# A block with deformable convolution and spectral filters: seven fills on GpSimd behind every 18 gathers

## What is computed

```python
n = layer_norm_over_channels(x)
# deformable convolution, 3x3, on n
offset = conv2d(n, offset_w, offset_b)            # 18 channels: where each tap looks
mask   = sigmoid(conv2d(n, mask_w, mask_b))       # 9 channels
# each tap reads four neighbours (y0,x0), (y0,x0+1), (y0+1,x0), (y0+1,x0+1) of a point
# that depends on the data, weighs them bilinearly and by the mask
out = einsum('bcthw,oct->bohw', val, weight)
out = batch_norm(out);  x = x + out * sigmoid(out)
# spectral filters on the tokens of layer_norm(x)
for i, frac in enumerate((1, 2, 4, 8)):           # four branches over the first 1/frac of the tokens
    U_plus, U_minus = causal convolutions of u with 16 filters
    si = sum_k sigma_k**0.25 * (U_plus M_plus[k] + U_minus M_minus[k]) + three lags of u by M_u
out = x + sum of the branches by a softmax choice
```

## Time and profile before

| | us |
|---|---|
| median of 3 runs | 725.98 |
| lowest and highest | 724.54, 726.33 |
| the profiled execution | 725.11 |
| its span, first instruction to last | 723.3 |

### The profile page before, as it was taken

One profiled execution on the slowest core, in us unless ns is written; L12 is line 12 of the kernel. 1 busy time (PEld: TensorE's weight loads), 2 busy tenths in 40 slices (PEclk: granted clock), 3 DMA queues, 4 the chain that ended last, 5 costly groups with the idle time before them and its releaser, 6 DMA issues.

```text
span 723.3 us, 9279 instructions
## 1 busy us (share of the span) xinstructions
PE 493.3 (68%) x3678; PEld 279.6 (39%) x3678; DVE 314.7 (44%) x800; ACT 167.6 (23%) x421; POOL 290.5 (40%) x295
## 2 busy tenths in 40 slices
PE   5977429334733983697459944997238636999998
PEld 3543104222522541254025611565125313565566
DVE  6468320749910980197006650079019701843000
ACT  1112003112401420241023300343024102433322
POOL 1157760450774277237710775007732771000000
PEclk9967557756865995699569965999659956999999
DMA  8525346830232133113310332003321331000000
GB/s 170 124 82 157 106 117 215 263 100 0 86 105 73 30 95 102 44 37 97 106 32 2 88 102 81 1 10 94 106 62 30 102 102 37 8 1 2 9 1 8
DMA packets 43763, 54.03 MB, mean 75 GB/s; under 512 B 24664, under 2 KB 34142, under 8 KB 43721
## 3 DMA queue, kind: packets, MB, share of 16 engines
q0 software_dynamic: 13824, 37.77, 18.0%
q1 hardware_dynamic: 23841, 13.42, 6.8%
q10 hardware_dynamic: 6056, 2.26, 1.3%
HBM read 50.12 MB, written 3.30 MB: 74 GB/s over the span
## 4 chain that ended last, share of the span: by engine, by line
PE 53%; issue 18%; another core or an unknown queue 18%; DVE 4%; ACT 4%; DMA 1%; SPq 1%; DVEq 0%
PE bank L891 28%; PE bank L903 7%; PE bank L836 3%; PE bank L762 2%; PE bank L826 2%; ACT u_conv L662 2%; PE bank L743 1%; PE bank L922 1%; PE bank L734 1%; PE bank L795 1%; PE bank L797 1%; DMA filt<-in_L_ffn_phi_dram 1%; PE bank L847 1%; DVE sil L468 1%
## 5 line engine op out<-in xcount | busy, mean ns | idle before, releaser
L269 POOL DMA_INDIRECT G<-corner_table,idx x288 | 287.9, 1000 | 310.0 <-DVE idx L362 191.3
L891 PE MATMUL bank<-filt,u_hi 128*64 128x512 f16 x1280 | 219.3, 405 | 55.8 <-issue 23.5
L662 ACT ACTIVATE u_conv<-bank,f_scale 128x256 f32<-128x256 f32 x256 | 106.0, 470 | 307.3 <-remote 159.6
L891 PE MATMUL bank<-filt,u_lo 128*64 128x512 f16 x640 | 142.0, 402 | 6.7 <-issue 6.2
L891 PEld LDWEIGHTS bank<-filt,u_hi 128*64 128x64 f16 x1280 | 80.3, 113 | 128.5 <-issue 48.0
L459 DVE TENSOR_TENSOR V<-G 128x576 f32<-128x576 f32 x32 | 24.3, 758 | 189.4 <-PE bank L827 111.6
L903 PE MATMUL bank<-u_conv,mixw 128*64 128x256 f32 (+1 forms) x640 | 87.1, 357 | 26.1 <-issue 25.9
L455 DVE TENSOR_TENSOR G<-G,bank 128x2304 f32<-128x2304 f32 x32 | 81.6, 2549 | 0.3
L903 PEld LDWEIGHTS bank<-u_conv,mixw 128*64 128x64 f32 x640 | 48.8, 144 | 50.7 <-issue 38.5
L891 PEld LDWEIGHTS bank<-filt,u_lo 128*64 128x64 f16 x640 | 43.3, 114 | 46.7 <-issue 19.1
L836 PE MATMUL bank<-vT,w_main 128*64 128x128 f32 (+1 forms) x320 | 26.2, 301 | 44.0 <-issue 40.9
(11 more groups left out here) (158 smaller groups left out, 369.8 us busy)
## 6 DMA issues: line engine op xcount, KB each, us to landing
filt<-filter_rows SPq DMA_DIRECT2D x16, 514.0 KB, 7.9
G<-corner_table,idx POOLq DMA_INDIRECT x288
corner_table<-n_uT SPq DMA_DIRECT2D x12, 128.0 KB, 2.8
mixw<-in_x_dram SPq DMA_DIRECT2D x2, 512.0 KB, 6.1
filt<-in_L_ffn_M_phi_plus_dram SPq DMA_DIRECT2D x8, 128.0 KB, 4.3
out_dram<-o_sb ACTq DMA_DIRECT2D x8, 128.0 KB, 1.9
filt<-n_L_ffn_M_phi_minus_dram ACTq DMA_DIRECT2D x4, 128.0 KB, 4.0
corner_table<-n_uT ACTq DMA_DIRECT2D x4, 128.0 KB, 2.8
```

The lines of the kernel that those rows point to most:

```text
L269: pool.indirect_dma_start(G[:, k, tap, :], None, corners[bp], bass.IndirectOffsetOnAxis(ap=idx[:, q % 2, k, tap:tap + 1], axis=0)).then_in ...
L662: act.activation(u_conv[:, g % 2, k, b2], conv_ps[b2][:, 2 * P * k:2 * P * k + 2 * P].rearrange("c (p a) -> c p a", p=2), ACT.Copy, scale= ...
L891: last = pe.matmul(conv_ps[b2][C * src:C * src + C, :].rearrange("c (k p a) -> c k p a", k=2, p=2), u[:, NJ * bp + j2, b2, src], h, start= ...
```

## The change

Behind the second and the fourth token row of each row q, which is behind 18 gathers each, GpSimd fills a new scratch tile of 128 x 1024 float32 with zeros, seven times. Each fill raises a semaphore, and GpSimd waits for it before the next instruction. That makes 16 times seven fills. Nobody reads the tile.

```diff
+REST, RESTS = 1024, 7
...
+        rest = sb("rest", [P, REST])
...
-        idx_ready = sem("idx_ready")
+        idx_ready, rested = sem("idx_ready"), sem("rested")
...
                                 G[:, k, tap, :], None, corners[bp],
                                 bass.IndirectOffsetOnAxis(ap=idx[:, q % 2, k, tap:tap + 1], axis=0)
                             ).then_inc(gathered[k], 16)
+                        if k % 2:
+                            for i in range(RESTS):
+                                pool.memset(rest[:], 0.0).then_inc(rested, 1)
+                                pool.wait_ge(rested, RESTS * (2 * q + k // 2) + i + 1)
```

## The result

| | before | after |
|---|---|---|
| median, us | 725.26 (4 runs, 721.93 to 726.33) | 697.75 (4 runs, 696.09 to 702.1) |
| ratio of the times, 95% interval | | 0.9637 [0.9582, 0.9693] |
| profiled execution, us | 725.11 | 696.97 |
| its span, us | 723.3 | 695.1 |
| mean granted clock | 0.787 | 0.801 |

The account below looks back on a forecast made before the run. Engines stand still while gathers run; 36% of the chain, about 260 us, shows no releaser. From 725.1 us: less 12 early stage, less 69 rows, plus 9 restarts gives 653; forecast 654 us, range 612 to 702.

Parts of the forecast that it names:

- The reading of what bounds the kernel: Some 19 us into a run of gathers, TensorE, VectorE and ScalarE are held nearly still (the hold); 177 us in six rows.
- The price of the pause: Seven waited fills on GpSimd take 7.7 us; with one issue gap the second 18 gathers come 8.0 us later.
- The second pause costs nothing: Behind k = 3, from 181 us on, the pause lies in GpSimd's wait for indices, 20.4 us at the shortest.
- The stage ahead: From 48.2 us to row 2's start at 181.05: GpSimd gets there at 160, at most 21 us gained, 12 taken.
- The rows: Six rows from 181 us on: two short holds, 18 us together, replace one of 29.5; 69 us back.
- How long there is the open number: How long engines run free into a row's second 18 gathers: 11.8 to 19 us, leaving 15.2 to 22.4 of hold.
- the restarts: Two a row instead of one, matmuls at 1.2 GHz behind each hold: 1.5 us a row, 9 us lost.
- the 4.36 us break ahead of 48.23: Early pause in gathers, after which engines ran at full pace until 60.0; source of the lower bound 11.8 us.
- Full relief: Rival: the pause empties everything, holds are 15.2 us a row, the early stage gives 21; 607 to 632 us, chance 0.18.
- The slower case: Rival: the hold returns as soon as gathers return, 4.7 to 8.0 us more per row; 767 to 798 us, chance 0.11.
- The fills hold VectorE: Rival: fills keep short VectorE operations waiting, 3.8 us for each of 15 pauses, 57 us; 680 to 710 us, chance 0.11.
- and vice versa: Skill rule that DMA and compute cannot slow each other; read as: gathers hold nothing, so a pause gives nothing.

Follow-up runs that it names:

- experiments 6 and 18: One waited fill of 160 elements behind every gather in place of the pauses, against the kernel before: 566.4 us (0.7802), on another chip 563.58 us (0.777).
- experiment 2: The pauses of rows q = 2 to 7 alone, without those of rows 0 and 1, against the kernel before: 715.83 us, 0.9823.
- experiment 3: The changed kernel with 14 fills in a pause instead of seven, against the kernel before: 735.63 against 728.49 us, 1.0134.
- Experiment 9: The kernel before with each gather fetching half of each partition's bytes, no fills: 742.71 against 742.16 us, one run.
- experiment 11: The changed kernel, waiting from row 2 on for four 4 KB SyncE copies instead of fills, against the kernel before: 755.75 us, 1.0175; void as a test.
- 15 to 17: The changed kernel with pauses of 14 fills of 450 elements, 25 of 180, or seven of 1024 again, against the kernel before: 0.9887, 0.9712, 0.9538.

## Why the prediction was right and wrong

**The reading of what bounds the kernel: right, in its form not quite.** The standstill goes with the gathers: with a fill between them that nobody reads, 1.47 us apart instead of 1.25, the long holds go and some 160 us with them (experiments 6 and 18). "What is held is every instruction, one by one" is too strong. In the held stretch from 60 us on VectorE's three long operations on a token row begin one right behind the other (86.07, 88.64, 90.03). And the short waits of a held stretch of before have a regular form that I had not seen:

```profile
82.10 0.15 DVE L291 SCALAR_TENSOR_TENSOR st<-st 64x1 f32<-64x1 f32 x1 [1.25 <-DVE st L290]
...
94.70 0.14 DVE L439 TENSOR_SCALAR f_max<-f_max 16x1 f32<-16x1 f32 x1 [1.25 <-DVE f_max L438]
96.10 0.15 DVE L440 RECIPROCAL f_max<-f_max 16x1 f32<-16x1 f32 x1 [1.26 <-DVE f_max L439]
98.20 0.74 DVE L443 TENSOR_SCALAR filt<-bank,f_max 16x512 f16<-16x512 f32 x1 [1.95 <-remote]
```

Where an engine has stood still, its next instruction begins a multiple of 0.70 us behind the one that was last held: 82.10 and 83.50 are 1.40 apart, 94.70 and 96.10 too, 96.10 and 98.20 are 2.10. TensorE's starts at 292.17, 294.97, 297.07 and 298.47 are 4, 3 and 2 times 0.70 apart, and in the kernel after those at 420.76, 422.17, 423.59, 425.69 and 428.49 are 2, 2, 3 and 4 times. The gathers' own distance, 1.25 us, is no such multiple.

**The price of the pause: right.** The first fill of a pause begins at 249.27 and the next gather at 256.57, 7.3 us where I had 8.0. The fill was 955 ns for 945; the gap between two fills was some 0.06 us ((7.03 - 7 x 0.955) / 6), not the 0.15 I had put in the middle of two bounds.

**The second pause costs nothing: right for four rows of five.** Behind the rows 2 to 5 GpSimd still waits for what comes after the pause (6.50 us at 225.57, 11.59 at 297.44). Row 7's first gather stands 0.27 us behind row 6's second pause (522.86): there GpSimd is the bound, in the shortest of the steps, 61.4 us.

**The stage ahead: right mechanism, half its size.** I had "at most 21 us gained", with GpSimd at row 2 at 160, and took 12 of them, because row 1's later gathers would now hold work that was free. They do: this window of the kernel after has 47 matmuls where the earlier trace rows have 162, but the one ahead of it has 189 for 28.

```profile
60.00:111.00 51.00, 39.93 (x189) 19.69 (x186) 35.03 (x84) 12.20 (x31) 41.54 (x43) 0.70 0.69 205
111.00:135.00 24.00, 8.64 (x47) 6.11 (x47) 19.62 (x64) 2.75 (x8) 19.73 (x21) 0.50 0.58 188
```

The bound itself was the answer: row 2 begins at 159.84, 0.27 us behind a fill. The term was 21.2 and not 12.

**The rows: the step that failed.** It is "How long there is the open number", with 19 us above and 11.8 below, and with it "A row has 15.2 to 22.4 us of hold". Measured were 7.4 and 8.3 us of free gathers behind the pause, and 26 and 30 us of hold in a row. With 7.4 in the prediction's own sum a row's hold is 7.6 + (22.5 - 7.4 + 4.1) = 26.8 us, 2.7 less than 29.5: six rows give 16 and the restarts take 9, so 7 us are left where the forecast had 60. The measured 7.0 is as near as that by luck: with the other row's 8.3 us the same sum gives 13, the late pauses alone gave 12.7 (experiment 2), the restarts were never measured, and two further terms missed in opposite directions. A first run isn't always free for 19 us (in the row at 373.20 it is 11.8), and the first hold of the row from 225.57 on ended 1 us behind its last gather (249.3; TensorE's groups are whole again at 250.23), where I had 4.1.

Two things were wrong with the number. I put my value nearer to the upper end because the pause was longer than the 4.36 us break ahead of 48.23: experiment 3 shows that in one row twice the pause brings 9.8 us and no more. And my lower bound came from that break, which lies behind nine gathers and not 18. Ahead of it there was a standstill too, but a short one. These are TensorE and ScalarE of the kernel before, and then of the kernel with 160 elements behind each gather:

```profile
34.51 4.57 PE L762 MATMUL bank<-filt,w_off 64*32 64x512 f32 x32
42.62 0.58 ACT L592 COPY filt<-bank 128x512 f32<-128x512 f32 x1 [8.35 <-remote]
```

```profile
34.80 4.52 PE L766 MATMUL bank<-filt,w_off 64*32 64x512 f32 x32
39.36 0.59 ACT L596 COPY filt<-bank 128x512 f32<-128x512 f32 x1 [4.97 <-PE bank L766]
```

The copy follows its matmuls at once in the second (39.32, 39.36) and 3.5 us late in the first (39.08, 42.62). So the break showed how long engines run behind a standstill of some 3.5 us that nine gathers made, and it was taken for how long they run behind 18 gathers and a hold of 8 us and more. That this is why 11.8 came out as 7.4 is likely and not shown.

**The restarts, 9 us:** not measured by themselves. TensorE's busy time rose by 15.4 us for the same matmuls, and the window behind the longer pause of experiment 3 has a granted clock of 0.74 (between the two levels of 1.2 and 2.4 GHz).

**The rivals.** *Full relief* failed with the same step. *The slower case* had its decision point at 4.7 us of free gathers; at 7.4 to 8.3 the change lies little above it, and it is the early stage that makes the result clear. *The fills hold VectorE* was a true mechanism of small size. The timeline of the kernel after shows three fills and two operations of VectorE beside them:

```profile
212.05 2.98 POOL L277 MEMSET rest<- 128x1024 f32 x3
213.08 0.97 DVE L292 TENSOR_SCALAR st<-st 128x2 int32<-128x2 int32 x1
214.08 0.97 DVE L293 TENSOR_SCALAR st<-st 128x2 int32<-128x2 int32 x1
```

```profile
215.09 0.16 DVE L295 SCALAR_TENSOR_TENSOR st<-st 128x2 f32<-128x2 f32 x1
215.28 0.16 DVE L296 TENSOR_TENSOR st<-st 128x2 f32<-128x2 f32 x1
```

The first two have a median of 0.17 us and take a whole fill; the next two, in the same pause, are not touched. VectorE's busy time rose by 9.7 us in all, 314.7 to 324.4, far from the 57 of that rival: the operations with two inputs in the chain that I feared for were not held. This is what the second half of the section "SBUF: two separate sides" in the Trainium skill's "SBUF — State Buffer" says: a VectorE operation in a two-port mode is blocked by any GpSimd one, one with two SBUF inputs only by a GpSimd operation that reads. The rows agree with it if a TENSOR_SCALAR runs in such a mode, which they don't tell.

The same section's "and vice versa" I had read as a rule against the change, and said the rows contradict it. Experiment 9 corrects that: with half the bytes moved the hold is the same, so nothing here shows transfers and engines contending at the memory, of which the sentence speaks, and the rows don't contradict it.

**Open.** What inside the chip the gathers' pace overloads, and why it clears at once for a few microseconds but not for long, no run shows: the time between gathers was changed here, not the thing they share with the other engines' instructions. Open too is what the 0.70 us between held starts are, whether idling relieves as filling does (experiment 11; every slower pace here was made with fills, so that a fill's own effect and the mere time can't be told apart), and whether each fill loads it as well (15 to 17).

## What to carry to other kernels

When idle time of all engines has no releaser in the profile, look for what runs evenly beside it, and change its pace before its volume: 0.22 us between gathers was worth 160 us, a pause of 7 us behind every 18th 28. A break behind a short congestion is no bound for what one behind a long congestion gives: take the bound from a recovery of the same size, or call it open. And where a stage is bound by one engine's own sequence, take its own sum as the value, not as the best case, unless a named wait stands in between.

## What the runs showed of the hardware

- Indirect DMAs issued back to back by GpSimd, 1.25 us apart, hold the instructions of TensorE, VectorE and ScalarE nearly still after some 6 to 21 us, with 1 KB for each of 128 partitions as with half the bytes (one run); for half the partitions, 1.21 us apart, after some 8 us (one run). At 1.34 us apart the kernel takes 0.92 of its time before, at 1.41 0.85, and at 1.47 and more no long holds are left (0.78).
- In a hold, starts of waiting instructions on all three engines lie multiples of 0.70 us apart.
- After a pause of 7 us the engines stayed free for 7 to 8 us of gathers, after one of 14 us for about 10 (two rows and one row looked at).
- A semaphore that GpSimd raises behind gathers can be up before they are issued: SyncE's copies ran some 12 gathers before the place at which the program asked for them (169.31, where the 18th gather began at 183.55).
- A memset of GpSimd can stretch a short TENSOR_SCALAR of VectorE from 0.17 to 0.97 us and leaves operations with two inputs at 0.16.
- The kernel before takes 742 us in two sets of runs and 724 to 728 in four, on different chips: each ratio needs its own chip's time.
